# Counting edge pairs in a graph kernel: byte casts of packed counts on GpSimd and ScalarE, out-degrees summed by TensorE, and a ring of 16 slots

## What is computed

```python
src = jax.random.randint(key, (50000,), 0, 3125)
dst = jnp.minimum((3125 * jax.random.uniform(key, (50000,)) ** 2.0).astype(jnp.int32), 99999)
_o = jnp.argsort(dst, stable=True); src = src[_o]; dst = dst[_o]
...
# first layer: edge_index = [src, dst]; row = src, col = dst
deg = jax.ops.segment_sum(ones, row, num_segments=N)
dinv_sqrt = jnp.where(deg > 0, jax.lax.rsqrt(deg_safe), 0.0)
w = dinv_sqrt[row] * dinv_sqrt[col]
h = jax.ops.segment_sum(w[:, None] * x[col], row, num_segments=N)
h = h @ W + b
...
x = _layernorm(x + _L0_gnn_ref(x, edge_index, ...))   # dense product with the counts
x = _layernorm(x + _L1_gnn_ref(x, src, dst, ...))     # attention over edges
x = _layernorm(x + _L2_gnn_ref(x, edge_index, ...))   # dense attention and three sums over neighbours
x = _layernorm(x + _L3_gnn_ref(x, weight, norm, src, dst, edge_type_16))
```

## Time and profile before

| | us |
|---|---|
| median of 3 runs | 3815.69 (3813.88 to 3818.88) |
| the profiled execution | 3814.58 |
| its span | 3812.8 |
| the stage `count_packed`, from its first slot to the landing of its last store | 87.3 to about 535 |
| first slot to closing 0 | 71.0 |
| closing 0 to closing 10 (tiles 1 to 10, 193 slots) | 186.0 |
| closing 10 to closing 23 (tiles 11 to 23, 137 slots) | 157.2 |
| closing 23 to the first load of the next stage at 541.2 | 39.7 |

### The profile page before, as it was taken

One profiled execution on the slowest core, in us unless ns is written; L12 is line 12 of the kernel. 1 busy time (PEld: TensorE's weight loads), 2 busy tenths in 40 slices (PEclk: granted clock), 3 DMA queues, 4 the chain that ended last, 5 costly groups with the idle time before them and its releaser, 6 DMA issues. The chain is left out here.

```text
span 3812.8 us, 46850 instructions
## 1 busy us (share of the span) xinstructions
PE 2943.8 (77%) x13253; PEld 2097.5 (55%) x13317; DVE 1841.9 (48%) x4590; ACT 875.8 (23%) x1237; POOL 1276.3 (33%) x929
## 2 busy tenths in 40 slices
PE   1777759774666666699999969999998999655565
PEld 1345537643555544466666658989894444344443
DVE  5999852355888887533233323434344221322223
ACT  0135644220100101022222224444441222000000
POOL 2000000007777740177667720000000000477776
PEclk9999979886677678899999989999999999778777
DMA  2046768314444421212222127666861444433334
GB/s 60 18 172 221 270 238 276 113 55 146 129 135 132 128 59 42 78 59 80 80 80 72 68 96 258 199 212 196 276 193 67 142 144 138 124 105 105 105 105 123
DMA packets 325254, 504.89 MB, mean 132 GB/s; under 512 B 27225, under 2 KB 238877, under 8 KB 317005
## 3 DMA queue, kind: packets, MB, share of 16 engines
q1 hardware_dynamic: 284477, 391.28, 30.5%
q0 software_dynamic: 40672, 112.31, 10.6%
HBM read 351.56 MB, written 152.75 MB: 132 GB/s over the span
## 5 line engine op out<-in xcount | busy, mean ns | idle before, releaser
L1791 POOL DMA_INDIRECT e7got<-rel_d,rel_i x416 | 394.6, 948 | 1139.9 <-POOLq L2699 1013.4
L1911 POOL DMA_INDIRECT a_got<-feat_d,src_i x416 | 404.1, 971 | 409.5 <-POOLq L2240 283.0
L1827 PE MATMUL e7sums<-e7got,e7hot 128*128 128x256 f32 x832 | 289.6, 508 | 197.0 <-DMA e7got<-rel_d,rel_i 166.4
L1425 PE MATMUL s_aggs<-s_blk_r,high 128*128 128x512 f32 (+1 forms) x1050 | 400.8, 382 | 20.7 <-DVE low L1544 20.5
L1425 PE MATMUL s_aggs<-s_blk_r,low 128*128 128x512 f32 (+1 forms) x1050 | 389.1, 371 | 0.0
L2740 PE MATMUL q_prods<-w,q_xt 128*128 128x512 f32 x800 | 352.8, 599 | 13.4 <-ACT q_xt L2760 13.4
L1827 PEld LDWEIGHTS e7sums<-e7got,e7hot 128*128 128x128 f32 x832 | 203.0, 255 | 280.4 <-issue 243.2
L1643 POOL TENSOR_SCALAR g_absent<-g_pairs 128x3200 bf16<-128x3200 f32 x25 | 274.8, 10992 | 171.4 <-DMA g_pairs<-pairs_d 171.3
L1690 PE MATMUL g_sums<-value,g_turned 128*128 128x257 f32 x1250 | 299.0, 383 | 8.6 <-ACT g_turned L1754 8.6
L1668 PE MATMUL g_scores<-key_t,g_q 128*128 128x512 f32 (+1 forms) x700 | 280.6, 556 | 19.9 <-DMA g_q<-query_d 13.3
L1799 DVE TENSOR_SCALAR e7hot<-iota,dloc,weight 128x128 f32<-128x128 f32 x416 | 115.7, 364 | 356.6 <-PE e7sums L1827 348.1
(11 more groups left out here) (422 smaller groups left out, 4469.7 us busy)
## 6 DMA issues: line engine op xcount, KB each, us to landing
s_blk<-turned_d SPq DMA_DIRECT2D x60, 1280.0 KB, 5.9
rel_d<-q_rows SPq DMA_DIRECT2D x25, 2048.0 KB, 7.5
s_blk<-turned_d SPq DMA_DIRECT2D x45, 960.0 KB, 5.1
pairs_d<-u_rows SPq DMA_DIRECT2D x25, 1600.0 KB, 8.1
turned_d<-u_line SPq DMA_DIRECT2D x25, 1600.0 KB, 7.1
g_pairs<-pairs_d SPq DMA_DIRECT2D x25, 1600.0 KB, 6.8
t_blk<-pairs_d SPq DMA_DIRECT2D x20, 1280.0 KB, 10.0
t_blk<-pairs_d SPq DMA_DIRECT2D x15, 960.0 KB, 5.1
```

What stands on the lines that cost most here:

```text
L1425: last = pe.matmul(aggs[:, idx % 2, half, 0:w], feats[l][part][:, a, half * P:(half + 1) * P], blk_r[:, q % RINGS, a % GA, 0:w], start=a = ...
L1791: pool.indirect_dma_start(got[:, j % U, :], None, table, bass.IndirectOffsetOnAxis(ap=index[:, j:j + 1], axis=0)).then_inc(arrived[j % U / ...
L1827: return pe.matmul(sums[:, 0:D], hot[:, u, :], got[:, u, :], start=False, stop=False)
L1911: pool.indirect_dma_start(got[:, n % 2, s, :], None, table, bass.IndirectOffsetOnAxis(ap=k.src_i[:, j:j + 1], axis=0)).then_inc(arrived[n ...
```

## The change

- VectorE's `take_apart` and its `closings` are gone, and so is `apart`. `whole` is read as bytes: its bytes 0 and 1 are cast into `rows` by ScalarE, byte 2 by GpSimd.
- `marks`, `tally` and `hist` are gone. TensorE sums the rows that it turns over: one product more in each of the seven groups of a closing (`sums`, 7 x 512), with float32r operands; the blocks are turned over by a float32r product with a unit matrix.
- The test for heavy degrees is another one: GpSimd casts byte 3 of `whole` (`above`) and adds it to `tops` in each tile. At the end VectorE reduces `tops`, and compares the sums of both degrees.
- The ring has 16 slots, and a turn of the loops on VectorE and TensorE takes 16 slots.
- `ready` has three constants to wait for, not four.

```diff
-    LOOK = 2
-    RING = 4 * LOOK
+    FOURS = 4
+    RING = 4 * FOURS
...
+            pool.memset(tops[:], 0.0).then_inc(summed, 1)
+            pool.wait_ge(summed, 1)
+            for t in range(T):
+                pool.wait_ge(copied, (t + 2) * COPIES)
+                if t >= 1:
+                    pool.wait_ge(summed, t + 1)
+                pool.tensor_copy(above[:], whole[:].bitcast(U8)[:, 3:4 * THIRD:4]).then_inc(topped, 1)
+                pool.wait_ge(flipped, (t + 1) * FLIPS)
+                if t >= 1:
+                    pool.wait_ge(stored, t * 16)
+                pool.tensor_copy(rows[:, 2 * THIRD:3 * THIRD], whole[:].bitcast(U8)[:, 2:4 * THIRD:4]).then_inc(spread_high, 1)
+                pool.wait_ge(topped, t + 1)
+                pool.tensor_tensor(tops[:], tops[:], above[:], ALU.add).then_inc(summed, 1)
...
+            step(dve.tensor_copy(ident_r[:], k.ident[:]))
...
-            dve.wait_ge(ready, 4)
+            dve.wait_ge(ready, 3)
-            eight(0, False)
-            with dve.Fori(1, S // 8) as i:
-                eight(i, True)
+            with dve.Fori(0, S // RING) as i:
+                for u in range(RING):
+                    j = i * RING + u
                     dve.wait_ge(used, j + 1)
                     dve.tensor_scalar(hot_d[:, u, :], k.iota_b[:], cols(k.dloc, j, 1), None, ALU.is_equal).then_inc(made, 1)
...
             def flip(closing, g):
                 pe.wait_ge(lined, closing * FLIPS + flip_room(g))
                 pe.sem_inc(k.passed, 1)
+                w = min(4, T - 4 * g) * P
+                pe.matmul(sums[0:FLIPS, 0:w], marks[:, g, :], rows[:, 4 * g * P:4 * g * P + w], start=False, stop=False)
                 for a in range(4 * g, min(T, 4 * g + 4)):
-                    last = pe.transpose(flips[:, g % 4, (a % 4) * P:(a % 4 + 1) * P], rows[:, a * P:(a + 1) * P], k.ident[:])
+                    last = pe.matmul(flips[:, g % 4, (a % 4) * P:(a % 4 + 1) * P], rows[:, a * P:(a + 1) * P], ident_r[:],
+                                     start=True, stop=True)
...
-                            pe.wait_ge(spread_out, t * 3 + 3)
+                            pe.wait_ge(spread_out, t * 2 + 2)
+                            pe.sem_inc(k.passed, 1)
+                            pe.wait_ge(spread_high, t + 1)
...
             def tile(t, b):
-                act.wait_ge(parted, t * 3 + 3)
+                    act.wait_ge(topped, t)
+                    act.wait_ge(spread_out, t * 2 + 2)
+                    act.wait_ge(spread_high, t + 1)
...
-                for part in range(3):
-                    act.wait_ge(parted, t * 3 + part + 4)
-                    act.copy(rows[:, part * THIRD:(part + 1) * THIRD], apart[:, part, :]).then_inc(spread_out, 1)
+                act.wait_ge(copied, t * COPIES + 2 * COPIES)
+                for part in range(2):
+                    act.copy(rows[:, part * THIRD:(part + 1) * THIRD], whole[:].bitcast(U8)[:, part:4 * THIRD:4]).then_inc(spread_out, 1)
```

More of the change, by code:

```diff
@@ L11 @@
 I32 = mybir.dt.int32
+U8 = mybir.dt.uint8
 ALU = mybir.AluOpType
@@ L782, in closings @@
[L782 to L787, removed]
-            def eight(i, closing):
-                for u in range(8):
-                    j = i * 8 + u
-                    if u % 4 == 0:
-                        if closing:
-                            closings((i * 2 + u // 4 - LOOK))
-                        marks(2 * i + u // 4, u // 4)
+            step(dve.tensor_copy(ident_r[:], k.ident[:]))
@@ L844, in _ @@
                 zeros(b)
-            pe.matmul(hist[:, 0:T], zero[0:EP, 0:P], zero[0:EP, 0:T], start=True, stop=False)
+            pe.matmul(sums[0:FLIPS, :], zero[:, 0:FLIPS], zero[:, 0:512], start=True, stop=False)
+            pe.wait_ge(marked, 1)
             def flip(closing, g):
@@ L885, in four @@
                                 flip(t, g)
-            with pe.Fori(0, S // 8) as i:
-                four(2 * i, 0)
-                four(2 * i + 1, 1)
-            pe.matmul(hist[:, 0:T], zero[0:EP, 0:P], zero[0:EP, 0:T], start=False, stop=True).then_inc(final, 1)
+            with pe.Fori(0, S // RING) as i:
+                for b in range(FOURS):
+                    four(FOURS * i + b, b)
             for n in range(BANKS):
@@ L893, in _ @@
             for closing in (T - 1, T):
-                pe.wait_ge(spread_out, closing * 3 + 3)
+                pe.wait_ge(spread_out, closing * 2 + 2)
+                pe.wait_ge(spread_high, closing + 1)
                 for g in range(FLIPS):
                     flip(closing, g)
-            pe.wait_ge(reduced, 1)
-            pe.transpose(hist[0:1, P:2 * P], largest[:, 0:1], k.ident[:])
-            pe.transpose(hist[0:1, 2 * P:3 * P], largest[:, 1:2], k.ident[:]).then_inc(laid, 1)
+            pe.matmul(sums[0:FLIPS, :], zero[:, 0:FLIPS], zero[:, 0:512], start=False, stop=True).then_inc(final, 1)
+            pe.wait_ge(given_in, 1)
+            pe.wait_ge(copied, (T + 1) * COPIES)
+            for a in range(4):
+                last = pe.transpose(counts[:, 1, a * FLIPS:(a + 1) * FLIPS], given[:, a * P:(a + 1) * P], k.ident[0:FLIPS, 0:FLIPS])
+            last.then_inc(upright, 1)
+            pe.wait_ge(checked, 1)
+            pe.matmul(counts[0:1, 0, 0:2], k.ones[:, 0:1], wrong[:], start=True, stop=True).then_inc(added, 1)
         @block.scalar
```

95 lines of the change are left out of this document (46 added, 49 removed).

## The result

The changed kernel takes 4301.90 us, median of four runs (4298.22 to 4304.92), beside 3817.19 of before (3813.88 to 3818.88): 1.127 times the time, 95% interval 1.125 to 1.129. The forecast was 3790, its range 3765 to 3835. The profiled execution has a span of 4303.1 us, 490 more than before. All medians of this document are those of fast executions: one of a_ring8_again, 5224 us at a granted clock of 0.554, is left out.

A forecast was written before the change was run, and what follows sets the result against it. VectorE was taken as the bound up to closing 10, sharing it with TensorE in late tiles. Gains of 18.8, 13 and 0 less 3 for clock and 3 at the end made 26 us: 3790, range 3765 to 3835.

The forecast's parts named there:

- part 6: Whole stage: adds VectorE's and TensorE's work, 18.8 + 13 + 0 - 3 - 3 = 26 us gained, hence 3790.
- rivals A to D: GpSimd holding VectorE up (3790, chance 0.52); slow casts (3815 or 3875, 0.25); cheap casts (3771, 0.15); GpSimd starved (3860, 0.08).
- 3 for the clock: TensorE's closings: at a lower granted clock they get dearer with more work in them, 3 us lost.
- part 1: VectorE: marks go, 80 us; taking apart goes, 52 us; its 22.6 us wait for ScalarE has no place left.
- part 2: GpSimd beside VectorE: each GpSimd operation holds VectorE up for its length less 0.15 us.
- part 3: GpSimd's operations per tile: two casts of 1.66 us and an add of 2.36, costing VectorE 5.2 us.
- rival C: GpSimd's casts cheap as a MEMSET or not holding VectorE up, so TensorE binds from tile 1: 3771 us, chance 0.15.
- the prediction's own rule: VectorE beside GpSimd: per tile it loses the three GpSimd operations' lengths less 0.15 us each.
- part 4: TensorE's closing: sums 1.45 us more, turning 0.2 less, marks' products 0.65 less; a late ten-slot tile costs 11.5 us.
- 5. ScalarE's casts: ScalarE casts two bytes, not three, 1.08 us less per tile; its 10.5 us cycle with the store stays below the others.
- 6. The end: After closing 23: sums and float32r at low clock cost 3 to 4 us, the cast returns 1; 3 lost.
- Rival D: GpSimd gets no turn between VectorE's gapless slots, so TensorE stands at closings of tiles 1 to 10: 3860 us, chance 0.08.

The follow-up runs named there:

- a_ring8_again: Second run of the changed kernel with a ring and loop turn of 8 slots, not 16: 3833.53 us, 1.0061 of before; the first run took 3835.95.
- b_pe16: Kernel before with only TensorE's loop written out over 16 slots instead of 8 (1,700 instructions): 4211.54 us, 401 over before.
- a_ring12: Changed kernel with ring and loops of 12 slots (1,441 instructions): 4146.23 us against 4169.06; run again on a second chip, 3799.97 against 3810.62.
- f_ring12_act3: Changed kernel with 12 slots and without GpSimd's three operations per tile; ScalarE casts the third byte, highest-byte test left out: 3791.60 us against 3810.62.
- e_dead: Kernel before with a never-run copy of both groups at the end of TensorE's loop body: 3828.22 us, 17.6 over before.
- a_short16: Changed kernel, ring of 16 kept, TensorE's loop written over 8 slots with the ring place from a register (1,076 instructions): 4021.26 us, 1.0558 of before.

## Why the prediction was wrong, step by step

**The step that failed** is one that the prediction made without a number. Its part 6 added up VectorE's and TensorE's work as if the loop's length had no price, and the rivals A to D had none with the code in it. The diff wrote TensorE's four groups out in one loop, and the program's own instruction count (852 to 1,920) was there to be read. The page's instruction queue, 54 packets in the kernel before, was not among the rows that I read. The result lies 467 us over the range, and b_pe16 shows 401 us for the length alone. The change's longer body is read in with 9.8 packets a turn, b_pe16's with 8.8; its closings are longer and run at the lower clock. How its further 100 us divide between the two was not measured.

**The sum without that step** is a_ring12, which has the same work and a ring of 12, and whose loop isn't read in again.

| | forecast | a_ring12_again | before |
|---|---|---|---|
| closing 0 at | 139.5 | 145.4 | 158.3 |
| closing 0 to 10 | 173 | 175.2 | 186.0 |
| closing 10 to 23 | 157.4 and 3 for the clock | 157.9 | 157.2 |
| closing 23 to the end of the stage | 3 lost | 44.2 | 39.7 |
| gain of the stage | 26 | 18.5 | |

1. Marks and taking apart (part 1): right. VectorE's slots follow each other in 0.62 us. But tile 0 gained 12.9, not 18.8: TensorE stood 3.10, 1.44 and 3.71 us at groups of the first turns, and the full ring held VectorE for it. From a_ring12_again:

```profile
95.11 3.59 PE L835 MATMUL u_counts<-u_hot_s,u_hot_d 128*128 128x512 bf16 x12 [3.10 <-DVE u_hot_s L790]
100.13 2.01 PE L835 MATMUL u_counts<-u_hot_s,u_hot_d 128*128 128x512 bf16 x12 [1.44 <-DVE u_hot_s L790]
105.85 18.13 PE L835 MATMUL u_counts<-u_hot_s,u_hot_d 128*128 128x512 bf16 x108 [3.71 <-issue]
107.04 0.25 DVE L789 TENSOR_SCALAR u_hot_d<-iota_b,dloc 128x128 bf16<-128x128 bf16 x1 [3.56 <-PE u_counts L835]
```

The slots were ready there (VectorE was up to 12 ahead). The queue has six packets from 90 to 107 us and none from 107 to 200 (11 from 81 to 520): in the loop's first turns the code comes in, and then it stays.

2. GpSimd holds up VectorE (part 2): right. From a_ring12_again, closing 10:

```profile
327.14 2.41 POOL L769 TENSOR_TENSOR u_tops<-u_tops,u_above 128x1042 f32<-128x1042 f32 x1
327.14 2.70 DVE L790 TENSOR_SCALAR u_hot_s<-u_places,u_column,u_value 128x1042 bf16<-128x1042 f16 x1
329.76 0.24 DVE L789 TENSOR_SCALAR u_hot_d<-iota_b,dloc 128x128 bf16<-128x128 bf16 x1
```

The same operation takes 0.55 us with GpSimd idle; this one ends 0.29 after the add.

3. The lengths (part 3): the add was 2.39 us in the changed kernel (forecast 2.36), the casts 1.05 instead of 1.66. That is the cheap end, rival C's value, and even under the MEMSET of as many columns that the changed kernel has (`u_tops`, 1.19 us). By the prediction's own rule such casts make 3.9 to 4.1 us. The loss is 2.9 us per tile, 402 us of `hot_d` and `hot_s` in a_ring12_again where 329 stood, forecast 5.2. Part of the rest can be seen at closing 10: GpSimd's second cast starts at 326.12, while VectorE waits for TensorE anyway (until 326.66). (No row shows the 0.1 us to start of the prediction's lengths; the add's two lengths, 2.39 us for 1042 columns and 6.95 for 3200, give 0.2.)

4. TensorE's closing (part 4): undersized. From a_ring12_again, the first rows of closing 10 at the full clock and the same of closing 11 at the lower one:

```profile
321.49 0.39 PE L854 MATMUL u_sums<-u_rows,u_marks 128*7 128x512 f32 x1 [0.65 <-issue]
321.71 0.56 PE L856 MATMUL u_flips<-u_ident_r,u_rows 128*128 128x128 f32 x4
...
334.98 0.63 PE L854 MATMUL u_sums<-u_rows,u_marks 128*7 128x512 f32 x1
335.41 0.95 PE L856 MATMUL u_flips<-u_ident_r,u_rows 128*128 128x128 f32 x4
```

From its first row to its last, a closing grew by 1.4 us at the full clock (5.4 from 4.0), forecast 1.25, but by 2.9 at the lower one (8.6 from 5.7). At the lower clock ran 3 of the first 10 and 3 of the next 13, one more in part. On average over these 23 it grew by 1.6 us. The prediction had 3 us in all for the lower clock. f_ring12_act3 shows what it means: with no GpSimd in the way, tiles 1 to 10 still take 172.3 us, where rival C had 157. The errors in 3 and 4 have opposite signs, and the 173 that came out was right by luck, with both its parts off.

5. ScalarE's casts from every fourth byte: 1.07 us each, as before. SyncE and the stores: pairs_d 10.7 us to landing in the changed kernel, nobody waits long for it.

6. The end: from closing 23 to the end of the stage a_ring12_again takes 44.2 us, the kernel before 39.7: 4.5 lost, forecast 3. Of these 3.6 lie between closings 23 and 24 (10.5 us from 6.9), 1 behind closing 24.

Small slips of the working: the sums' 3200 columns make 1.42 us, not 1.45, and rival C's gain in tiles 11 to 23 is 4.5 (157.2 less 152.7), not 3. Neither moves a chance.

So the sum of what the prediction priced came out near, 18.5 for 26, though two of its prices were off in opposite ways (2.9 us for 5.2 beside GpSimd, and a closing at the lower clock 2.9 for 1.25); and what it didn't price was worth some 500: the stage of the changed kernel ends at 1024.6, that of a_ring12 at 522.7. Rival D didn't come up: in a_ring12_again GpSimd's cast starts at 322.19, 0.06 us after the cast of `whole` ends.

Open are the difference of 8 us between a_ring12_again's time (10.6 gained) and its stage (18.5), since before was not traced on that chip, the cause of the granted clock's changes from run to run (a_ring8 had 0.70 from 350 to 400 us, a_ring12 0.91 from 300 to 400), and how the 16 us of a turn beyond VectorE's 10 divide between the wait for packets and the slower clock behind the gaps. A ring of 16 with a body of at most 1,567 instructions and fixed addresses was not tried.

## What to carry to other kernels

Count the instructions of a loop's body ahead of unrolling it, engine by engine and weight loads included, and look at the instruction queue's packets on the page: packets in proportion to the turns, with idle time at the loop's turn that nothing ends, mean that the engine waits for its own code. Price every delay against the ring that is to swallow it: the same work of GpSimd's cost 3 us of the stage with 12 places and some 26 with 8. And where one engine is busy 96% of a stretch, read the second engine's cycle too before a gain on the first one is counted.

## What the chip showed that I had not expected

- A TensorE loop of up to 1,567 instructions isn't read in again between its turns; with 1,700, used all over, it is, each time, with 8.8 packets of 16 KB and 7 us at the loop's turn. The 2048 instructions that the Trainium skill gives ("Runtime: NRT & Kernel Launch", "Instruction fetch mechanics") are over the edge that these runs show. The same section of the Trainium skill says that a taken branch out of a window of two blocks forces a fetch. These runs don't show that either: bodies of 3 to 6 blocks turned 52 and 34 times with 54 to 60 packets in the whole program.
- A stretch of 845 instructions at the end of the body that is never run doesn't bring the fetching: e_dead spans 1,697 instructions and shows 57 packets. Code between used pieces is another matter (b_pe16).
- The gaps come with a lower clock: with them TensorE is granted 0.65 to 0.68, and twelve products take 3.69 us there instead of 2.0. It is the smaller part: the products of the slots keep TensorE busy 285.2 us instead of 211.7, 74 more, beside 334 of gaps.
- GpSimd casts 1042 bytes, each from every fourth place, to float32 in 1.05 us, 1.0 ns a column: under its MEMSET of 1042 columns (1.19 us) and well under its one-input step L203 (2.3 ns a column, 1.5 without the assumed start).
- With TensorE operands whose place comes from a register, four slots of three products took 4.05 us of TensorE, with fixed places 2.0 (a_short16, a_ring12_again). That the registers are the reason is likely, not shown apart.
